# Linear attention stage: a list schedule with each engine's part placed by itself, fixed state buffers, inputs loaded a block ahead

## The reference

```python
q = relu((x @ Wq.T)) + EPS          # 16 heads of 16, per token
k = relu((x @ Wk.T)) + EPS
v = x @ Wv.T
kv_cum = cumsum(einsum('bhsd,bhsm->bhsdm', k, v), axis=2)
out = einsum('bhsd,bhsdm->bhsm', q, kv_cum)
k_cum = cumsum(k, axis=2)
z = 1.0 / (einsum('bhsd,bhsd->bhs', q, k_cum) + EPS)
out = (out * z[..., None])          # heads joined to (b, s, 256)
x = layernorm(x + out @ Wo.T)
```

## Time and profile before

| | us |
|---|---|
| median of 3 runs | 3028.58 |
| lowest, highest | 3028.43, 3034.52 |
| profiled execution | 3030.09 |
| its span, first to last instruction | 3028.3 |
| TensorE busy in the span | 2859.1 (94%) |
| DVE, ACT, POOL busy | 2171.4, 1611.7, 1049.2 |

### The profile page before, as it was taken

One profiled execution on the slowest core, in us unless ns is written; L12 is line 12 of the kernel. 1 busy time (PEld: TensorE's weight loads), 2 busy tenths in 40 slices (PEclk: granted clock), 3 DMA queues, 4 the chain that ended last, 5 costly groups with the idle time before them and its releaser, 6 DMA issues.

```text
span 3028.3 us, 52408 instructions
## 1 busy us (share of the span) xinstructions
PE 2859.1 (94%) x20384; PEld 1934.4 (64%) x20384; DVE 2171.4 (72%) x5057; ACT 1611.7 (53%) x2976; POOL 1049.2 (35%) x1210
## 2 busy tenths in 40 slices
PE   7898999999999999999998799999999899999997
PEld 5676886533343333333334678888888788888886
DVE  6777345677778778777884677777776577887874
ACT  2221332454655555555565566666667566666662
POOL 3333342113212411221142344444454453444441
PEclk9999999999999999999999899999999999999998
DMA  3000001131322032122212000000010000000001
GB/s 103 2 2 2 28 4 20 18 38 12 37 24 27 6 43 22 17 26 33 25 39 75 24 5 4 5 5 5 12 32 15 27 26 5 12 11 12 11 11 58
DMA packets 46795, 66.63 MB, mean 22 GB/s; under 512 B 10174, under 2 KB 34772, under 8 KB 46548
## 3 DMA queue, kind: packets, MB, share of 16 engines
q1 hardware_dynamic: 46548, 63.29, 11.8%
HBM read 24.99 MB, written 8.39 MB: 11 GB/s over the span
## 4 chain that ended last, share of the span: by engine, by line
PE 72%; DVE 15%; DMA 5%; ACT 3%; POOL 2%; issue 1%; SPq 1%; POOLq 0%; ACTq 0%; DVEq 0%
PE ps L1274 16%; PE pw L121 12%; PE ps L121 10%; PE pw L1250 9%; DMA e_hs<-x 4%; PE ps L1054 4%; PE ps L1434 4%; PE pw L1054 3%; DVE a_am L1770 3%; PE pw L1347 2%; PE pw L1385 2%; PE ps L1238 1%; PE pw L1204 1%; PE pw L1367 1%; DVE stat L1713 1%
## 5 line engine op out<-in xcount | busy, mean ns | idle before, releaser
L1559 ACT ACTIVATE c_p<-pw 128x1024 f32<-128x1024 f32 x512 | 522.6, 1021 | 429.4 <-PE ps L1238 350.6
L1846 DVE TENSOR_REDUCE c_mx<-ps 128x1 f32<-128x512 f32 x1024 | 658.5, 683 | 123.2 <-PE ps L1238 119.8
L1274 PE MATMUL ps<-c_p,c_v 128*64 128x512 f32 x2048 | 555.1, 620 | 7.8 <-DVE c_mr L1859 7.3
L1238 PE MATMUL ps<-c_kst,c_qst 48*128 48x512 f32 x1024 | 386.0, 451 | 6.9 <-DMA c_kst<-shared 3.5
L1250 PE MATMUL pw<-c_qst,c_kst 50*128 50x512 f32 x1024 | 377.0, 447 | 0.8 <-DVE c_v L1819 0.8
L1250 PEld LDWEIGHTS pw<-c_qst,c_kst 50*128 50x128 f32 x1024 | 152.3, 185 | 314.3 <-issue 302.0
L1612 ACT ACTIVATE e_sm<-e_sm,e_mx 128x256 f32<-128x256 f32 x512 | 253.8, 498 | 62.2 <-DVE e_mx L1990 61.9
L2110 POOL TENSOR_SCALAR stat<-stat 128x1 f32<-128x1 f32 (+1 forms) x138 | 31.2, 226 | 719.0 <-DVE stat L1716 429.5
L121 PE MATMUL pw<-shared,e_xb 128*128 128x512 f32 x792 | 218.0, 414 | 2.3 <-DVE e_xb L1939 1.6
L2215 POOL TENSOR_TENSOR e_ss<-e_ss,half 128x16 f32<-128x16 f32 x64 | 186.8, 2918 | 87.3 <-DVE e_ss L1947 70.1
L1274 PEld LDWEIGHTS ps<-c_p,c_v 128*64 128x64 f32 x2048 | 103.0, 135 | 165.8 <-issue 128.3
(11 more groups left out here) (309 smaller groups left out, 6137.6 us busy)
## 6 DMA issues: line engine op xcount, KB each, us to landing
c_qst<-shared SPq DMA_DIRECT2D x192, 64.0 KB
c_kst<-shared SPq DMA_DIRECT2D x192, 64.0 KB
x<-in_L_attn_x SPq DMA_DIRECT2D x8, 512.0 KB, 8.7
keep<-x SPq DMA_DIRECT2D x8, 512.0 KB, 4.5
e_raw<-keep SPq DMA_DIRECT2D x8, 512.0 KB, 3.5
out<-x SPq DMA_DIRECT2D x8, 512.0 KB, 5.9
e_hs<-x SPq DMA_DIRECT2D x64, 63.5 KB
e_raw<-in_L_ffn_w SPq DMA_DIRECT2D x10, 248.0 KB
```

What stands on the lines that cost most here:

```text
L1238: e.matmul(bank_of("c_max", n, sh, qt, h), c_qst[i][p0:p0 + 48, sh // 2, 128 * qt:128 * qt + 128], c_kst[i][p0:p0 + 48, sh // 2, 512 * h:5 ...
L1274: ins = e.matmul(pv[64 * h:64 * h + 64, :], c_v[b % 2][:, kt, 33 * hd:33 * hd + 64], p[:, 512 * h:512 * h + 512], start=kt == 0, stop=kt = ...
L1559: e.activation(c_p[kt % 2][:, :], wides[slot["c_s", (n, sh, kt)]], ACT.Exp, scale=0.5).then_inc(SC, 1)
L1846: e.tensor_reduce(c_mx[m % 2][:, qt, h:h + 1], bank_of("c_max", n, sh, qt, h), AX.X, ALU.max).then_inc(VE, 1)
```

## The change

`plan_a` is written anew. The scheduler of stage d becomes the class `Order`, which both stages use; it gets a time lag per releasing engine (0.22 us behind TensorE, 0.06 behind others in stage a) and a cost `turn` of 0.05 us for a TensorE step whose tile shape is not that of the step before. Each engine's part of each step is an operation with its own due time (DUE_A, plus 8.4 us for each chunk) and duration (TOOK). The state buffers are fixed: chunk ch writes a_st[(ch + 1) % 3] and reads a_st[ch % 3], and the waits on the ring become waits on a_out of two chunks before. x i is requested when the second a_q product of block i - 1 is done. The a_const step is split into the DMAs (a_const) and the memsets (a_ones). Stage d gets the same schedule from the class as from its own functions. Of the diff, with what the prediction speaks of:

```diff
+        "pe a_x": 0.46, "act a_x": 0.6, "dve a_x": 0.69, "pe a_q": 1.5, "dve a_q": 0.65, "pool a_qz": 2.6, "pe a_kv": 1.5,
+        "dve a_kv": 0.42, "act a_kv": 0.4, "pe a_kt": 0.24, "act a_kt": 0.4, "pe a_state": 0.3, "dve a_state": 0.84,
+        "pool a_sum": 1.3, "pe a_am": 1, "dve a_mask": 0.68, "pe a_out": 2, "act a_out": 0.57, "pe a_ot": 0.44,
+        "dve a_ot": 0.83, "pe a_at": 0.24, "act a_at": 0.38, "dve a_at": 0.42, "pe a_wo": 0.95, "dve a_wo": 0.47,
+        "dve n_st a": 0.6, "pool n_st a": 0.8, "dve n_nm a": 0.42}
...
+PACE_A, NEAR_A = 8.4, 0.06
+DUE_A = {"pe a_x": -30, "act a_x": -30, "dve a_x": -30, "pe a_q": -24, "dve a_q": -24, "a_qz": -10, "pe a_kv": -4,
+         "dve a_kv": -4, "act a_kv": -3, "pe a_kt": 4, "act a_kt": 4, "pe a_state": 5, "dve a_state": 6, "a_sum": 6,
+         "pe a_am": 10, "dve a_mask": 11, "pe a_out": 16, "act a_out": 16, "pe a_ot": 20, "dve a_ot": 20, "pe a_at": 24,
+         "act a_at": 24, "dve a_at": 24, "pe a_wo": 28, "dve a_wo": 28, "dve n_st": 32, "pool n_st": 32, "dve n_nm": 36}
...
+    def starts(self, o):
+        t = max(o["from"], self.engine_at[o["eng"]] + self.turn * (o["eng"] == "pe" and o["mode"] != self.mode))
+        for r in {id(r): r for r, *_ in o["takes"]}.values():
+            c = sum(q is r for q, *_ in o["takes"])
+            if len(r.idle) < c:
+                return 1e9
+            t = max(t, self.room_at(r.idle[c - 1]))
+        return t
+
+    def run(self, until):
+
+        P, ready = self.P, self.ready
+        while ready:
+            times = [self.starts(o) for o in ready]
+            first = min(times)
+            if first >= until:
+                return
+            t, _, k = min((o["due"], k, k) for k, o in enumerate(ready) if times[k] <= first + self.eps)
+            o, t = ready.pop(k), times[k]
...
+            order = Order(P, NEAR_A, {"pe": 0.22}, 0.06, 0.05)
...
+            for i in range(1, 8):
+                moved(33 * (i - 1) - 20, f"x{i}", 1, "x_in", (i,), [("pe", "a_q", i - 1, 1)], lasts=5.0)
...
+                    op(at(ch, "act a_x"), "act", "a_x", i, 1, [("pe", "a_x", *i)] +
+                       ([("pe", "a_kv", ch - 5), ("pe", "a_q", bk - 2, 1)] if bk > 1 else []))
...
+                put("pe", "a_am", after=[("act", "a_kt", ch), ("pool", "a_qz", ch)], takes=[(bank, "a_am", ch, r) for r in range(4)], mode="rows")
                 for r in range(4):
+                    put("dve", "a_mask", r, after=[("pe", "a_am", ch)] + ago(2, "pe", "a_out") + [("dve", "a_mask", ch, r - 1)] * (r > 0),
+                        gives=[(bank, "a_am", ch, r)])
+                state = ago(1, "pool" if (ch - 1) % 8 else "dve", "a_sum" if (ch - 1) % 8 else "a_state") if old else []
+                put("pe", "a_out", after=[("act", "a_kv", ch), ("dve", "a_mask", ch, 3)] + state + [("pe", "a_state", ch)] * more +
+                    ago(1, "pe", "a_out"), takes=[(bank, "a_out", ch)], mode="cols")
...
             def a_state(ch):
-                b, new, old = bank_of("a_state", ch), a_st[slot["a_st", (ch + 1,)]], ch % 8 != 0
+                b, new, old = bank_of("a_state", ch), a_st[(ch + 1) % 3], ch % 8 != 0
...
-                if old:
-                    w.wait_ge(*pool("a_sum", ch - 2))
-                else:
-                    for s in room["a_st", (ch + 1,)]:
-                        w.wait_ge(*of(s[0], s[1], tuple(s[2:])))
+                w.wait_ge(*pool("a_sum", ch - 2 if ch % 8 > 2 or not old else ch - 4))
+                if not old:
+                    w.wait_ge(*pe("a_out", ch - 2))
...
             def x_in(i):
+                w.wait_ge(*pe("a_q", i - 1, 1))
                 e.dma_start(x[:, 4 * i:4 * i + 4, :], xin[:, 4 * i:4 * i + 4, :]).then_inc(sems[f"x{i}"], 16)
```

More of the change, by code:

```diff
@@ L284, in plan_a @@
         def plan_a():
[L285 to L292, removed]
@@ L293, in plan_a @@
-            weight_out(raws, "a_wo")
-            for i in range(1, 8):
-                P.land(f"x{i}", 1, "x_in", i)
-                P.add("x_in", i)
-            bank, state = Ring(range(8)), Ring(range(3))
-            def chunk(ch):
[L300 to L316, removed]
-                for r in range(4):
[L318 to L346, removed]
+            raws, bank = Ring(range(2)), Ring(range(8))
@@ new lines, in plan_a, with at, moved, place @@
+            order = Order(P, NEAR_A, {"pe": 0.22}, 0.06, 0.05)
+            op = order.op
+            def at(ch, key):
+                return PACE_A * ch + DUE_A[key]
+            def moved(due, name, count, kind, i, after=(), takes=(), before=None, lasts=3.0):
+                def place(t):
+                    if before:
+                        before()
+                    P.land(name() if before else name, count, kind, *i)
+                    P.add(kind, *i)
+                    order.over_at["dma", kind, i] = t + lasts
+                    order.settle([("dma", kind, i)])
+                op(due, "sp", kind, i, 1, after, takes, place=place, took=0.7)
@@ new lines, in fetch, with place @@
+            def fetch(due, key, hi, lo, src, scale, by, width):
+                def place():
+                    weight(key, a_raw[slot["w_in", (key,)]], hi, lo, [(slice(0, 128), src)], scale, by)
+                i = (key,)
+                moved(due, lambda: f"raw_a{slot['w_in', i]}", 1, "w_in", i, (), [(raws, "w_in", key)], place)
+                here = ("dma", "w_in", key)
+                if scale is not None:
+                    op(due, "dve", "w_out", i, 1, [here], took=width * 0.8)
+                    here = ("dve", "w_out", key)
+                op(due, "act", "w_out", i, 1, [here], took=width)
+                op(due, by[1], "w_out", i, 1, [("act", "w_out", key)], gives=[(raws, "w_in", key)],
+                   took=width * (2.5 if by[1] == "pool" else 1.1))
@@ L348, in plan_b @@
+            for bk in range(8):
+                block(bk)
+            for ch in range(NT):
+                chunk(ch)
+            order.run(1e8)
+            assert not order.blocked and not order.ready, (list(order.blocked)[:9], [(o["eng"], o["kind"], o["i"]) for o in order.ready])
         def plan_b(bank, between):
@@ L654, in plan_d @@
             tqs = Ring([0])
[L655 to L707, removed]
-                    else:
[L709 to L713, removed]
+            order = Order(P, EPS, {}, LAG)
@@ L716, in fetch @@
+            op, settle, run, room_at = order.op, order.settle, order.run, order.room_at
+            over_at, engine_at, blocked, ready = order.over_at, order.engine_at, order.blocked, order.ready
             def fetch(due, key, hi, lo, src, after):
@@ L1476, in a_x @@
                 w.wait_ge(*pe("a_kv", 4 * bk - 5))
+                w.wait_ge(*pe("a_q", bk - 2, 1))
                 w.wait_ge(*pe("a_x", bk, k))
```

113 lines of the change are left out of this document (104 added, 9 removed).

## The result

The kernel after takes 2985.65 us at the median of four runs (2984.02 to 2988.65), the kernel before 3028.51 in the same comparison. The ratio is 0.9857, with a 95% interval from 0.984 to 0.9874: 42.9 us less, where 22.7 were forecast and 2996 was the lower end of the range. The direction was right, the size was not.

What follows compares the result with a forecast made beforehand. TensorE was taken to bound stage a, with 12% idle time, mostly waits on masks. Gains of 3.3 (start) and 19.4 us (waits) sum to 22.7, forecasting 3006 us, range 2996 to 3020.

Steps and rivals of the forecast that it cites:

- Part 1: Start of the kernel: x copies ahead of the weight copies let q start at 9.5 us; gain 3.3 us, bounds 2 to 4.
- Part 2: TensorE's waits on masks in stage a: idle share falls to stage d's, busy time unchanged; gain 19.4 us.
- Part 3: Inputs requested a block ahead: price 0, only block 1's x could hold TensorE once, 0 to 3 us.
- Part 4: Fixed state buffers and new waits in stage a: cost 0, bounds 0 to 2 us; no bank seen missing.
- Part 5: Clock in stage a: first slow stretch may vanish, second stays; taken as 0, bound 2 us of gain.
- rival 1: Stage a's list packs better than stage d's, 1% idle, no slow clock early; 32.7 us gain, 2996 us; chance 0.17.
- Rival 2: Stage a's pace stays near the list's own 8.4 us a chunk; gain 10.1 us, 3018.5 us; chance 0.17.
- Rival 3: Waits move from masks to other steps, x 1 takes back the start's gain; 3028 us, no change; chance 0.05.
- Rival 4: DVE runs other steps between a chunk's four masks, so a_out comes later; slower, 3047.7 us; chance 0.06.
- The sum's bounds: Whole kernel: range of the forecast time, 2996 to 3020 us, taking in two rivals and the smaller parts' bounds.

Runs made afterwards that it cites:

- e3: Kernel before, order untouched, each mask multiplying only 32 of 128 columns per head; 2987.07 us (one run).
- e7: Kernel after with 0.02 instead of 0.05 us in the list for a change of tile shape; 2992.28 us (one run).
- e4: Kernel after, but x 1 to 7 requested together behind the first weights, as before the change; 2990.92 us, ratio 0.988 to before.
- e2: Kernel before with one turn more between masks and a_out, six chunks active instead of five; 3035.85 us, ratio 1.0035.
- e1: Kernel before with only the two steps that split the first x moved ahead of the three weight splits; 3028.95 us (one run).
- e10: Kernel after with 9.0 us a chunk in the due times instead of 8.4; 2984.58 us (one run).
- e11: Kernel after with 8.2 us a chunk in the due times instead of 8.4; 2980.46 us, ratio 0.9849 to before.
- e12: Kernel after with its list rebuilt of whole steps, each at its TensorE part's place, only the masks at places of their own; 3079.20 us (one run).
- e9: e4 with the list told that the first two FFN weights take 14 us instead of 3; 2984.15 us (one run).

## Why the prediction was wrong

The reading of the bound was right: TensorE with 34.4 us of idle time in the stage, 28.5 of them on masks, filled by an order that puts other work ahead of a_out. Of the steps:

- **Part 1** said 3.3 us and q at 9.5; it is 3.4 and 9.40.
- **Part 2 is the step that failed, in two terms.** The first is the busy time, "I take as unchanged: no matmul is added or removed". It fell by 11.8 us. Three things are in it, and only the first is measured cleanly. The stalls: 4.7 us in the middle five blocks by e3, 0.24 for each of 20; with the 11 waits outside at up to that price it is 5 to 7 (an estimate). The slow clock: the stretches of the earlier trace rows ran at 0.66 and 0.57, the stage after at 1.00 from 25 to 30 us and 0.98 from 240 to 259.4; step by step against the same steps at full clock (a_out's halves in the tail 2.08 and 1.94 us for 1.16 and 1.08) the slow stretches cost 4.5 us. The changes of shape: some 1.6 by e7. The busy share of a row was taken for work. It is the union of overlapping matmuls whose ends are modelled, and by e3 each stall adds to it. The Trainium skill says it plainly (Trainium Kernel Development and Optimization, Performance Expectations): "matmul busy time (the `TensorMatrix` row) is a bad metric for how close a kernel is to roofline, because matmuls are pipelined", and names the weight loads' busy share as a good one. Here the loads' time stayed from before to e3 (121.96 and 121.59 us in five blocks) where the matmuls' fell by 4.7. It is not a constant of the work either: over the stage it is 198.81 us before, 195.93 in e3 and 192.27 with the new order.
- The second term is the idle time left. I took stage d's 3.1%, 8.1 us, for the stage and 6.8 for its tail, and it is 7.26 in all: the tail and almost nothing else. Stage d's idle time is its own. Its largest row there is 13.3 us in nine waits behind one DVE step (e_qn), which says nothing about a stage with no such chain. The two terms, 11.8 and 7.7 (14.9 less 7.26), are the 19.5 us between 269.5 and 250.0.
- **Part 3**: 0 to 3 us for block 1's x was right in result, and TensorE waited for no x behind the first. But the price of the opposite choice, 8.9 us by e4, came from a queue that I had named (SP's, with the FFN weights behind it) and not followed to who waits for them.
- **Part 4**: no wait of TensorE's on a state buffer shows in the stage. Banks were hardly a limit here (0.5 us, the scores for a mask); they are where the waits land once DVE is late (e2, e4).
- **Part 5** took 0, bounded the gain at 2 us and said that the second slow stretch stays. Both went, and they cost 4.5 us. The first stretch, some 1.6 us, went in e1 too. The second went as well: the tail still has its idle time (6.5 of 11.4 us busy from 248 on), but the clock there stays near 1.00, and only stage b's first products run slow.
- **The rivals**: rival 1 (2996) was nearest and still 10 us short, since it too held the busy time at 254.56. Rival 2 took a constant of the list for a pace; e10 and e11 show that it is none. Rival 3 didn't come. Rival 4 was real as a mechanism (e12) and didn't happen here, where one rule places all parts of the list.
- **The sum's bounds** were too narrow in just the way of part 2: the upper bound of its gain was "nothing idle but the tail", 27.5 us, with no bound for what a stall costs beyond its idle time. From q to stage b the gain was 38.9 us.

## What to carry to other kernels

Price a wait of TensorE in the middle of dense work at its idle time and about a quarter of a microsecond more, and look at the granted clock behind it: here, in e3, 28 us of waits were worth 38, some 3 of them the clock's. To learn what an order can bring, thin out the work that is waited for and leave the order alone, as in e3; it gave the stage's new length within 1 us from q on, before any scheduling. And in a list laid by durations every queue trusts each of them: one load that lands late stops all that stands behind it on its engine, and to mix two rules of placing in one engine's list, as e12 did, can cost more than either rule alone.

## What the runs showed of the hardware

- A stall of TensorE cost 0.24 us of its busy time beside the idle time (20 stalls in five blocks, 31.03 against 30.08 us a block), at full clock: 0.15 in the step ahead of it and 0.08 in the one that waited.
- Waits of up to 1.4 us inside dense work left the granted clock at 1.00 in the earlier trace rows, while longer ones (4.5 us in e4) and a cluster at the start were followed by steps at half of it: the second half of a_out behind it took 1.94 us in e4 for 1.08.
- The part from stage b on, the same instructions in the same order, took from 2721.4 to 2731.5 us in the fourteen profiled executions above. What moves it is the clock: behind stage b's start the records have the lower level for 93 us in e4 and e9 (2721.5 and 2721.4 us), 105 before (2726.6), 109 after (2727.1) and 117 in e1 (2731.5), and the other runs lie between, in nearly the same order. Why the same instructions get the lower level for longer in one execution stays open.
